# A scan's last sums taken ahead of the rate maxima, a border-only clear moved ahead of a norm, and zero products on TensorE before two norms

## The reference, cut to what matters

```python
x = x + attention(gn(x))                 # 6 heads over 1024 pixels
x = x + gelu(layernorm(scan4(gn(x))))    # a selective scan in four directions
x = x + topk_mask(conv3x3(gn(x))) * gn(x) # depthwise; 30 largest scores of a channel keep their pixel
x = x + mix(gn(x))                       # projection, depthwise conv, chunked state space, projection
```

## Time and profile before

| | us |
|---|---|
| runs, median of 3 | 12510.87 |
| runs, lowest and highest | 12497.52 and 12556.97 |
| profiled execution, whole | 12547.2 |
| profiled execution, span of its instructions | 12545.4 |
| PE, busy | 10024.8 (80%) |
| DVE, busy | 8217.2 (65%) |
| POOL, busy | 7729.8 (62%) |
| ACT, busy | 4364.8 (35%) |

### The profile page before, as it was taken

One profiled execution on the slowest core, in us unless ns is written; L12 is line 12 of the kernel. 1 busy time (PEld: TensorE's weight loads), 2 busy tenths in 40 slices (PEclk: granted clock), 3 DMA queues, 4 the chain that ended last, 5 costly groups with the idle time before them and its releaser, 6 DMA issues. The chain is left out here.

```text
span 12545.4 us, 91862 instructions
## 1 busy us (share of the span) xinstructions
PE 10024.8 (80%) x28440; PEld 2891.6 (23%) x28440; DVE 8217.2 (65%) x7943; ACT 4364.8 (35%) x5374; POOL 7729.8 (62%) x3710
## 2 busy tenths in 40 slices
PE   6787878878778787878878778787878878778787
PEld 1112122122222212122122222212222122222212
DVE  2367666666766666666666766667666666766666
ACT  1243333423334243333424334243333424334243
POOL 0384756838567483756838567483856848566583
PEclk9697888979788897878879788787878979788897
DMA  0352542524335152543524335252533524345252
GB/s 14 89 123 63 122 109 69 123 68 115 88 89 142 49 123 60 125 106 73 122 69 116 83 96 135 53 119 60 127 105 73 126 66 118 81 100 131 56 122 57
DMA packets 358663, 1181.05 MB, mean 94 GB/s; under 512 B 67483, under 2 KB 68747, under 8 KB 358023
## 3 DMA queue, kind: packets, MB, share of 16 engines
q1 hardware_dynamic: 331703, 1157.28, 37.0%
q10 hardware_dynamic: 24800, 15.62, 0.5%
q0 software_dynamic: 1520, 0.78, 0.1%
HBM read 1004.06 MB, written 156.02 MB: 92 GB/s over the span
## 5 line engine op out<-in xcount | busy, mean ns | idle before, releaser
L1235 POOL TENSOR_TENSOR arena<-arena 128x1024 f32<-128x1024 f32 x1536 | 3664.8, 2401 | 740.5 <-issue 718.1
L1251 POOL TENSOR_TENSOR arena<-arena 128x1024 f32<-128x1024 f32 x1152 | 2714.7, 2357 | 1358.3 <-DVE arena L1190 1355.7
L1016 PE MATMUL ps<-arena,sel_y 128*32 128x512 f32 x6144 | 3317.2, 675 | 200.1 <-POOL arena L1251 177.4
L1190 DVE TENSOR_TENSOR_SCAN arena<-ps,arena 128x1024 f32<-128x1024 f32 x1152 | 2628.1, 2281 | 659.1 <-ACT ps L1128 640.8
L1128 ACT ACTIVATE ps<-arena,v_na 128x1024 f32<-128x1024 f32 x1536 | 1716.6, 1118 | 3466.6 <-DVE arena L1190 2393.1
L917 DVE TENSOR_REDUCE arena<-ps 128x1 bf16<-128x512 f32 x1632 | 1113.1, 682 | 1321.6 <-PE ps L700 1321.6
L869 ACT ACTIVATE arena<-ps 128x512 f32<-128x512 f32 x1632 | 880.2, 591 | 846.9 <-PE ps L725 846.5
L1016 PEld LDWEIGHTS ps<-arena,sel_y 128*32 128x32 f32 x6144 | 602.9, 118 | 2405.1 <-issue 2016.6
L1180 DVE TENSOR_TENSOR_SCAN ps<-ps,arena 128x1024 f32<-128x1024 f32 x384 | 879.7, 2291 | 383.1 <-ACT ps L1128 324.4
L700 PE MATMUL ps<-arena 32*128 32x512 bf16 x1632 | 676.9, 415 | 474.0 <-DVE arena L917 474.0
L725 PE MATMUL ps<-arena 33*128 33x512 f32 x3264 | 994.0, 688 | 73.5 <-ACT arena L832 55.0
(11 more groups left out here) (217 smaller groups left out, 11915.7 us busy)
## 6 DMA issues: line engine op xcount, KB each, us to landing
arena<-scan_dtu SPq DMA_DIRECT2D x770, 512.0 KB, 6.1
arena<-scan_dt SPq DMA_DIRECT2D x770, 512.0 KB, 4.7
arena<-scan_bc SPq DMA_DIRECT2D x260, 512.0 KB, 6.7
scan_dt<-arena SPq DMA_DIRECT2D x68, 512.0 KB, 8.1
scan_dtu<-arena SPq DMA_DIRECT2D x68, 512.0 KB, 4.8
scan_dt<-arena SPq DMA_DIRECT2D x68, 256.0 KB, 4.1
scan_dtu<-arena SPq DMA_DIRECT2D x68, 256.0 KB, 4.8
XN<-arena SPq DMA_DIRECT2D x204, 64.0 KB, 4.2
```

The source lines that it names most:

```text
L1016: mm = nc.tensor.matmul(ps[3][32 * q:32 * q + 32, HALF * h:HALF * h + HALF], sel_y[:, r, :], step[:, i % NBUF, HALF * h:HALF * h + HALF], ...
L1190: nc.vector.tensor_tensor_scan(step[:, i % NBUF, o], ps[2][:, o], step[:, i % NBUF, o], 0.0, ALU.mult, ALU.add).then_inc(m_h, 1)
L1235: pool.tensor_tensor(step[:, i % NBUF, :], dur[:, i // 2 % DUR, :], Bb[2 * (k // 2) + f], ALU.mult).then_inc(m_bu, 1)
L1251: pool.tensor_tensor(step[:, i % NBUF, :], step[:, i % NBUF, :], Cb[2 * (k // 2) + f], ALU.mult).then_inc(m_hcp, 1)
```

## The change

It has four parts.

1. The tail of the scan on DVE: one maximum (unit 0) stays ahead of the last sums, units 1 and 2 follow them, units 3 and 4 come after the centring, and unit 5 moves behind the statistics of norm 2, into a new argument `meanwhile` of `norm_dve`.
2. On POOL product 5 moves behind `norm_pool(pool, 2)`.
3. The clears of the mix become a function of their own, `mix_clear`, that clears only the borders of `CP` (two instructions instead of one) and stands ahead of `norm_pool(pool, 3)`. The counts in the waits on `b_z` grow by one each.
4. On PE eight products of zeros are added ahead of `norm_pe(pe, 2)`, once two of the four additions to `X` are done (`m_x`), and eight ahead of `norm_pe(pe, 3)`, once the convolution's result is added (`k_x`).

```diff
-        def norm_dve(dve, u, writes, x_in=X, begun=False, room=None):
+        def norm_dve(dve, u, writes, x_in=X, begun=False, room=None, meanwhile=None):
 
             norm_sums(dve, u, x_in, begun)
+            if meanwhile is not None:
+                meanwhile()
             norm_var(dve, u)
...
-            setup_dve(dve, range(0, 4))
+            setup_dve(dve, range(0, 1))
             taken(3)
+            setup_dve(dve, range(1, 3))
...
-            setup_dve(dve, range(4, 6))
+            setup_dve(dve, range(3, 5))
...
         def mix_act(act):
             act.wait_ge(f_out, 1)
-            act.wait_ge(b_z, 2)
+            act.wait_ge(b_z, 3)
...
-            dve.wait_ge(b_z, 3)
+            dve.wait_ge(b_z, 4)
...
-        def mix_pool(pool):
+        def mix_clear(pool):
             pool.wait_ge(f_out, 1)
             pool.wait_ge(k_x, 2)
-            pool.memset(CP[:, :, :], 0.0).then_inc(b_z, 1)
+            pool.memset(CPv[:, :, 0:PAD:PAD - 1, :], 0.0).then_inc(b_z, 1)
+            pool.memset(CPv[:, :, 1:1 + H, 0:PAD:PAD - 1], 0.0).then_inc(b_z, 1)
             pool.memset(prev[0:32, 0, :], 0.0).then_inc(b_z, 1)
             pool.memset(dAR[:, :, :], 0.0).then_inc(b_z, 1)
+
+        def mix_pool(pool):
             pool.wait_ge(b_zc, 4)
...
                     scan_pe(pe, front_pe(pe))
+                    pe.wait_ge(m_x, 2)
+                    keep_clock(8, bank(6))
                     norm_pe(pe, 2)
                     conv_pe(pe)
+                    pe.wait_ge(k_x, 2)
+                    keep_clock(8, bank(6))
                     norm_pe(pe, 3)
                     keep_clock(16, bank(6))
...
-                    norm_dve(dve, 2, lambda t, n: XPv[0:n, t, 1:1 + H, 1:1 + W], begun=True, room=k_z)
+                    norm_dve(dve, 2, lambda t, n: XPv[0:n, t, 1:1 + H, 1:1 + W], begun=True, room=k_z,
+                             meanwhile=lambda: setup_dve(dve, range(5, 6)))
...
                     conv_pool(pool)
-                    setup_pool(pool, range(2, 6))
+                    setup_pool(pool, range(2, 5))
                     norm_pool(pool, 2)
+                    setup_pool(pool, range(5, 6))
+                    mix_clear(pool)
                     norm_pool(pool, 3)
                     mix_pool(pool)
```

## The result

The changed kernel takes 12337.93 us (median of 4 runs, 12300.52 to 12339.44) against 12533.92 us for the kernel before in the same comparison (median of 4, 12497.52 to 12561.12): a ratio of 0.9836, 95% interval 0.9815 to 0.9858. That is 196 us or 1.6% less; forecast were 12410 us, 101 us less, 0.8%. The time lies inside the range of 12335 to 12470, at its lower edge, and the gain is about twice the one forecast.

The account below looks back on a forecast made before the run. No engine is busy throughout; each image's tail is a chain of waits between engines. 7.2 - 2.2 + 1.3 = 6.3 us an image, times 16 = 101 us, gives 12410 us (0.8% less), range 12335 to 12470.

Parts of the forecast that it names:

- The last sums: Scan's tail: sums straight behind PE's last pass bring the scalings forward; 7.2 us an image gained, bounds 6.7 and 14.0.
- the higher of the two cases: Clock stays up in the scan's norm: scalings start 14.0 us earlier, three wait for POOL's products; gain 7.7 us.
- the one with a low clock: Clock falls anyway in the scan's norm, its 16 passes cost as now: scalings start 6.7 us earlier.
- Product 5: Norm 2's first write on DVE waits for this POOL product: 2.2 us an image lost, bounds nothing and 3.3.
- The clears: Norm 3: border clears ahead of the power cost nothing; DVE's four writes take 1.91 us, but sixteen zero products are late.
- the 1.3 us of part 4: Norm 3: eight zero products start PE 3 us earlier, some of the sixteen run at full clock; 1.3 us gained.
- my upper bound of 3.6: Norm 3: all sixteen zero products at twice the low-clock rate end at 1103.5, a gain of 3.6 us.
- The 0.4 us that I charged: Norm 3: added zero products run until 1098.0, statistics are ready at 1097.63, so group sums start late: 0.4 us lost.
- Its lower end: Scan's tail: only one of three products meets the scalings; 10.8 us an image, 173 us, 12338, say 12335.
- The first (no hindrance): Scalings on DVE and products on POOL pass each other: 13.1 us an image, 210 us, 12301 us; chance 0.14.
- The second: Maxima 1 and 2 wait for products ahead of the centring: 3.2 us an image, 51 us, 12460 us; chance 0.18.
- The third: Clock falls over the group sums, mix projections run at 1.0 us a pass: 84 us slower, 12595 us; chance 0.04.

Follow-up runs that it names:

- `after`: The changed kernel with all four parts of the change, against the kernel before: 12337.93 us, ratio 0.9836.
- `last_sums_alone`: The kernel before with only the last sums moved ahead of maxima 1 to 5; products, clears and zero products as before: 12410.19 us, ratio 0.9903.
- `zero_products_alone`: The kernel before with only the two groups of eight zero products added, ahead of norms 2 and 3: 12584.65 us, ratio 1.0074.

## Why the prediction went right and wrong

**The last sums: right.** They start at PE's last pass, the clock stays up through mean and variance (the higher of the two cases: 8.66 us for 16 passes), and the scalings start 14.1 us earlier, forecast 14.0. They meet products 2 to 4 as forecast and end at 25.9 us after the last scan step; the sum's own times put it at 1038.2 - 1012.2 = 26.0. I had then taken 7.2 between this case and the one with a low clock, and 7.8 came. Only the form was wrong. I had three of four scalings wait for one product each. In fact one scaling waits for all three, 7.01 us. The three clears of before did the same to the write of 5.11 us. The form that I had forecast is there too, in the kernel with the last sums alone: one wait of about 2.1 us at each of three products. So the total came out right with a form that this kernel doesn't have, which is partly luck; what decides between the two forms is open. The Trainium skill ("SBUF — State Buffer", "Who interferes with whom"), which the prediction cites, says that the engine which comes second blocks for the whole of the other's instruction. The rows of the last sums alone agree, with 2.82 us beside products of 2.77; the 7.01 us row shows a wait through three, which goes beyond it.

**Product 5: right,** +2.0 us against +2.2. The experiment shows that a shift behind the writes doesn't avoid it; one behind the taps does.

**The clears: right as far as the sum took them.** 1.9 us in four instructions beside the statistics, the writes at 1.91, and alone they bring 1.1 us.

**The step that failed is the 1.3 us of part 4.** I let the eight products start PE 3 us earlier, noted that the clock of before rose only 8 us after PE's start, and concluded that only some of the sixteen would run at the full clock. In the changed kernel the clock rises 2.8 or 3.6 us after PE's start on the eight, so the group sums and all sixteen run at 2.4 GHz. 4.2 us came instead of 1.3, near my upper bound of 3.6 for the sixteen plus 0.8 for the sums. Leaving the eight out takes 2.6 of the 4.2 away. I had read one image for the time of the rise and taken it for all. The kernel before itself has two: 8.0 us after PE's start in eight images, 6.7 in the other eight. The other runs show that the eight lift the clock in time or not depending on the image, so one delay could not carry the term. The 0.4 us that I charged for sums that start later was more than made up in the changed kernel: from the statistics to the variance it takes 1.6 or 1.9 us, against 2.23 before. As a loss it came only where the eight failed to lift the clock, with 2.75 us in such images of the other runs.

**Small terms that I had at nothing:** 0.35 us between the scalings and norm 2's statistics (before, DVE waits there for the gelu; behind the held-up scalings it doesn't); 0.4 us in norm 2, where the eight lift the clock in time in half of the images; and 1.1 us in the mix, through the moment of the clock's fall.

**The range.** Its lower end stood for a case in which two of three products miss the scalings, 10.8 us an image. The tail's gain is 10.8 us too, but all three products met the scalings, and the excess came from norm 3. That the time lies inside the range is luck.

**The rivals.** The first (no hindrance) didn't come. The experiment with products behind the taps shows what it would have given: 6.3 us more up to the end of the scalings (19.6 instead of 25.9), where the prediction had 6.8. The second didn't come: DVE went first for maximum 2. The third, with 0.04, didn't come here, but its outcome is real: it came in 7 of 16 images once the clears were put back behind the power, by a pause and not by the group sums. In the changed kernel the moved clears leave no such pause. I hadn't seen that the clears' move protects against what the zero products can do, so that the low chance fitted for a reason other than mine.

## What to carry to other kernels

On an in-order queue, put what others wait for ahead of what nobody waits for yet, and give the leftovers a place beside work that they don't hold up, as the top 30 here; a move to the next neighbour can just move the wait (2.0 us at the writes became 2.1 at the first tap). Filler products that lift PE's clock should run until the real work starts: here a filler that ended 3.7 us early was worse than none, since the clock then fell on the work it was meant for. Before you say what filler is worth, look at the same place in many passes of the loop, and at the moment of the clock's rise in each. Where it falls into two kinds, longer filler that starts earlier was worth more here than an exact fit.

## What the runs showed of the hardware that I had not expected

- A VectorE instruction with two operands in SBUF that came 0.46 us behind the first of three back-to-back GpSimd products waited for all three: 7.01 us instead of 0.68 (`after`, 7.0 in all 16 images). With four such products in a row that came while VectorE was busy, VectorE got its turn after each: 2.82 us for each of three instructions (`last_sums_alone`, all 16 images). What decides isn't shown.
- A pause of TensorE of 3.70 us in front of the projections went with 22.58 us for 24 passes, one of 2.32 us with 12.51 us; the window behind the first reads 0.50, that behind the second 1.00 (`zero_products_alone`).
- Eight zero products, 3.2 to 3.6 us of work, lifted the clock by the start of the group sums or during them in all 16 images of the changed kernel, in 13 of 16 with clears and zero products, in 11 with products behind the taps, and in 7 and 11 of the two kernels with the old clears. The work was the same within each kernel; the moments at which the clock had fallen before it were not.
- In the changed kernel's trace, clearing 256 elements a partition in 128 pairs, 33 elements apart within a pair, took 455 ns on POOL, and 272 in eight rows took 327 ns; in the kernel before 4624 in one piece took 3951 ns.
